# An LSTM step with a top-2 mixture of experts on one core: first half of expert 2's low weights added by DMA two token tiles sooner, two powers moved by a tile, a load and an output half on ScalarE's queue

## What is computed

```
def step(carry, xp_t):
    h_prev, c_prev = carry
    g = xp_t + h_prev @ u
    gates = jax.nn.sigmoid(g[:, :3 * H])
    c_cand = jnp.tanh(g[:, 3 * H:])
    ...
    c = fg * c_prev + ig * c_cand
    h = og * jnp.tanh(c)
x = _layernorm(x + _L0_attn_ref(x, w, u, bias), axis=-1)
...
dispatch, combine = _gating_top2(logits, C)
expert_inputs = jnp.einsum('GSEC,GSM->EGCM', dispatch, x)
layer_w0 = jnp.einsum('EGCM,EMH->EGCH', expert_inputs, w0_kernel)
layer_w1 = jnp.einsum('EGCM,EMH->EGCH', expert_inputs, w1_kernel)
hidden = jax.nn.gelu(layer_w0, approximate=True) * layer_w1
expert_outputs = jnp.einsum('EGCH,EHM->EGCM', hidden, wo_kernel)
out = jnp.einsum('EGCM,GSEC->GSM', expert_outputs, combine)
x = _layernorm(x + out, axis=-1)
```

## Time and profile before

| | us |
|---|---|
| median of 3 executions | 337.28 |
| lowest, highest | 336.99, 338.23 |
| the profiled execution | 338.06 |
| its span in the profile (first to last instruction) | 335.9 |
| busy in the span: PE, DVE, ACT, POOL | 287.1, 251.5, 217.8, 186.3 |
| mean granted clock of PE, as a share of full speed | 0.93 |

### The profile page before, as it was taken

One profiled execution on the slowest core, in us unless ns is written; L12 is line 12 of the kernel. 1 busy time (PEld: TensorE's weight loads), 2 busy tenths in 40 slices (PEclk: granted clock), 3 DMA queues, 4 the chain that ended last, 5 costly groups with the idle time before them and its releaser, 6 DMA issues.

```text
span 335.9 us, 5632 instructions
## 1 busy us (share of the span) xinstructions
PE 287.1 (85%) x1676; PEld 240.0 (71%) x1676; DVE 251.5 (75%) x805; ACT 217.8 (65%) x498; POOL 186.3 (55%) x154
## 2 busy tenths in 40 slices
PE   8999999968622996329999999999999999999990
PEld 5666665658611886229999987877888888889890
DVE  2799989987501894027888889989877777999985
ACT  4687987877421573026777876876765666669884
POOL 5015888788775027787864444347347337368700
PEclk9999999998985699557999999999999999999996
DMA  7996294478751005334444336264324224523664
GB/s 226 361 406 191 68 239 138 131 153 247 168 179 47 19 27 150 104 36 46 50 65 58 51 49 176 50 145 57 48 22 56 34 23 86 114 22 40 95 187 132
DMA packets 46828, 37.74 MB, mean 112 GB/s; under 512 B 7073, under 2 KB 40800, under 8 KB 46800
## 3 DMA queue, kind: packets, MB, share of 16 engines
q1 hardware_dynamic: 35392, 26.56, 26.8%
q0 software_dynamic: 11408, 10.85, 21.0%
HBM read 17.86 MB, written 17.10 MB: 104 GB/s over the span
## 4 chain that ended last, share of the span: by engine, by line
PE 71%; DVE 13%; issue 7%; another core or an unknown queue 5%; ACT 3%; ACTq 0%; POOL 0%; DVEq 0%; POOLq 0%
PE big L676 12%; PE big L674 12%; PE big L675 11%; PE big L582 5%; PE b_xnt L690 3%; PE b_xnt L693 3%; PE b_xnt L691 3%; PE b_ht L693 3%; PE b_ht L690 2%; PE b_ht L691 2%; PE b_rt L710 2%; PE b_xt L626 2%; PE big L568 1%; PE b_ht L631 1%
## 5 line engine op out<-in xcount | busy, mean ns | idle before, releaser
L878 ACT ACTIVATE act_g<-big 128x256 f32<-128x256 f32 (+1 forms) x144 | 65.4, 454 | 88.9 <-PE big L676 57.6
L674 PE MATMUL big<-x_hi,e_hi 128*128 128x256 f32 (+1 forms) x264 | 88.8, 336 | 4.1 <-issue 3.8
L675 PE MATMUL big<-x_hi,e_lo 128*128 128x256 f32 (+1 forms) x264 | 86.0, 326 | 0.0
L676 PE MATMUL big<-x_lo,e_hi 128*128 128x256 f32 (+1 forms) x264 | 86.0, 326 | 0.0
L511 POOL DMA_INDIRECT slots<-rows,slot_ix x64 | 66.3, 1035 | 35.5 <-issue 18.6
L526 POOL DMA_INDIRECT tokens<-contrib,token_ix x32 | 52.0, 1625 | 38.6 <-DVE token_ix L1169 30.6
L526 POOL DMA_INDIRECT tokens<-zero_rows,token_ix x28 | 45.6, 1629 | 32.9 <-DVE token_ix L1169 25.8
L674 PEld LDWEIGHTS big<-x_hi,e_hi 128*128 128x128 f32 x264 | 52.0, 197 | 8.0 <-issue 3.5
L676 PEld LDWEIGHTS big<-x_lo,e_hi 128*128 128x128 f32 x264 | 51.7, 196 | 4.0
L675 PEld LDWEIGHTS big<-x_hi,e_lo 128*128 128x128 f32 x264 | 52.0, 197 | 3.4
L1177 DVE TENSOR_TENSOR h<-act_g,big 128x256 f32<-128x256 f32 (+3 forms) x36 | 18.3, 509 | 18.8 <-ACT act_g L878 13.7
(11 more groups left out here) (212 smaller groups left out, 683.9 us busy)
## 6 DMA issues: line engine op xcount, KB each, us to landing
e_raw<-in_L_ffn_w_kernel_dram SPq DMA_DIRECT2D x16, 320.0 KB
slots<-zero_rows SPq DMA_DIRECT2D x8, 548.0 KB, 8.1
e_lo<-e_raw POOLq DMA_DIRECT2D x5, 544.0 KB
e_raw<-in_L_ffn_wo_kernel_dram SPq DMA_DIRECT2D x8, 320.0 KB
xd<-slots SPq DMA_DIRECT2D x16, 137.0 KB
xd<-slots SPq DMA_DIRECT2D x8, 274.0 KB
x<-in_L_attn_input_seq_dram SPq DMA_DIRECT2D x8, 256.0 KB, 4.6
tokens<-rows SPq DMA_DIRECT2D x8, 256.0 KB
```

What stands on the lines that cost most here:

```text
L674: pe.matmul(dst, e_hi[q][:, c0:c0 + m], xdt_hi[u % 2][:, 0:w], start=True, stop=False)
L675: pe.matmul(dst, e_lo[q][:, c0:c0 + m], xdt_hi[u % 2][:, 0:w], start=False, stop=False)
L676: mm = pe.matmul(dst, e_hi[q][:, c0:c0 + m], xdt_lo[u % 2][:, 0:w], start=False, stop=True)
L878: nc.scalar.activation(act0[n % RH][0:m, 0:w], pre(n, P)[0], ACT.Gelu_apprx_tanh).then_inc(gelu_ready, 1)
```

## The change

Five edits, by where they stand:

- On POOL the power of group 5 is issued two scatters later (before tile (1, 2) instead of (1, 1)), and the power of group 7 two scatters sooner (before (1, 5) instead of (1, 6)). The half of expert 2's low part that is made by DMA is issued four scatters sooner (before (1, 5) instead of (1, 7)).
- That half is now the first one (pieces 0 and 1), and DVE makes pieces 2 and 3. So ACT negates piece 0 in LSTM step 6 and piece 1 after chunk 4 of unit 0, instead of pieces 2 and 3 after chunk 5 of unit 0. DVE's first subtraction stays in LSTM step 7 (for piece 2 instead of 0); its second (piece 3, was 1) moves from after chunk 2 of unit 0 to after chunk 1 of unit 1.
- The load of `w_raw` is issued by ACT instead of SP.
- The outputs of groups 6 and 7 are stored in halves. SP stores the first half of 7, the first of 6 and the second of 7; ACT stores the second half of 6.
- Nothing is computed in another way, and PE's own list of instructions is the same.

```
-    NEGATIVE = {2: [(0, 0), (0, 1)], 4: [(1, 0)], 5: [(1, 1), (1, 2), (1, 3)]}
+    NEGATIVE = {2: [(0, 0), (0, 1)], 4: [(1, 0)], 5: [(1, 1), (1, 2), (1, 3)], 6: [(2, 0)]}
-    LOWS_AMONG = {(0, 3): (0, 1), (1, 2): (1, 0), (1, 3): (1, 1), (1, 7): (2, 1)}
-    ROOTS_AMONG = {(0, 3): 2, (0, 5): 3, (0, 7): 4, (1, 1): 5, (1, 3): 6, (1, 6): 7}
+    LOWS_AMONG = {(0, 3): (0, 1), (1, 2): (1, 0), (1, 3): (1, 1), (1, 5): (2, 0)}
+    ROOTS_AMONG = {(0, 3): 2, (0, 5): 3, (0, 7): 4, (1, 2): 5, (1, 3): 6, (1, 5): 7}
...
+        def half_out(g, h):
+
+            return out[g].rearrange("(t p) d -> p t d", p=P)[:, h * T // 2:(h + 1) * T // 2, :]
+
+        def half_fin(g, h):
+
+            return fin[g][:, h * T // 2:(h + 1) * T // 2, :]
...
-            sp.dma_start(w_raw[:, :], w_in[:, :]).then_inc(w_loaded, 16)
...
-            for g in range(S):
+            for g in range(LAST):
                 sp.wait_ge(fin_ready[g], T)
                 sp.dma_start(out[g].rearrange("(t p) d -> p t d", p=P), fin[g][:, :, :]).then_inc(out_done, 16)
-            sp.wait_ge(out_done, 16 * S)
+            for h in range(2):
+                for g in range(S - 1, LAST - 1, -1):
+                    if g == S - 1 or h == 0:
+                        sp.wait_ge(fin_ready[g], T // 2 * (h + 1))
+                        sp.dma_start(half_out(g, h), half_fin(g, h)).then_inc(out_done, 16)
+            sp.wait_ge(out_done, 16 * (S + GB))
...
+            act.dma_start(w_raw[:, :], w_in[:, :]).then_inc(w_loaded, 16)
...
-                    if (u, k) == (0, 5):
+                    if (u, k) == (0, 4):
+                        negative_weights(2, 1)
+                    elif (u, k) == (0, 5):
                         high_weights(2, 3)
-                        for n in range(PIECES // 2, PIECES):
-                            negative_weights(2, n)
...
+            act.wait_ge(fin_ready[LAST], T)
+            act.dma_start(half_out(LAST, 1), half_fin(LAST, 1)).then_inc(out_done, 16)
...
-                    low_weights(2, 0)
+                    low_weights(2, 2)
...
             chunk(0, 2)
-            low_weights(2, 1)
             chunk(0, 3)
...
             chunk(1, 1)
+            low_weights(2, 3)
             chunk(1, 2)
```

## The result

| | before | after |
|---|---|---|
| median of 20 executions each, us | 337.68 | 340.75 |
| ratio, with its 95% interval | | 1.0088 (1.0056 to 1.012) |
| profiled execution, us | 338.06 | 339.61 |
| its span, us | 335.9 | 337.5 |
| mean granted clock of PE | 0.93 | 0.926 |

A forecast was written before the change was run, and what follows sets the result against it. PE was taken as the bound except in two holes ending with POOL's scatter trains. POOL's 1.45 us plus 0.5 us at the end, 1.95 us off 337.28, gave 335.3 us, range 332.4 to 339.8.

The forecast's parts named there:

- The step that failed: PE's two idle stretches, about 84 to 109 and 126 to 151 us, were taken to end with POOL's scatter trains.
- the sum built on it: 1.45 us on POOL plus 0.5 us at the end, 1.95 us off the 337.28 median, giving 335.3 us.
- the rival "slower": POOL's train of 22 scatters, from about 76.6, opens the first hole sooner: 339.6 us, chance 0.20.
- the two signs: ACT's "remote" waits begin in unit 1, or PE's first dense stretch starts after 109.3 us.
- 4.3 us gross: 5.5 us of units 1 and 2, worth 4.4 chunks, would yield one: 3.4 chunks lost.
- The end: Final output stores: last issue 0.4 us sooner and half as large; 0.5 us gained, from 0.2 to 0.8.
- The start: Load of w_raw from ACT: SP's later loads some 0.45 us sooner, put at 0, range 0 to 0.4 us.
- POOL's shift: Power 5 no longer waits, so POOL's first scatter train ends 1.45 us sooner, between 1.1 and 1.8.
- unit 2 no longer held by `wait_low`: Expert 2's half lands by 82 us, so PE's 2.87 us idle before unit 2 at 88.90 goes.
- POOL did not wait for ACT's negation: Rival: POOL waits for ACT's piece 1 before issuing expert 2's half; 1 us of it gives 336.3, chance 0.04.
- the excess of its neighbours: Scatter beside power 5 took 0.52 us over the usual 0.98; if it and its neighbour lose this, about 1.8 us gained.
- The half of expert 2, put at nothing beyond POOL's shift: Issue moves from 82.37 to about 75.5; worth between nothing and 2.87 us, put at nothing since POOL sets the hole's end.

The follow-up runs named there:

- cutting that train once: Whole change plus one unused POOL power (1.16 us) ahead of tile (1, 7): 0.9977 of the kernel before.
- the kernels with pauses: Unused 1.1 us POOL powers ahead of every second tile of batches 2 and 3: changed kernel 0.916 and 0.9113, kernel before 0.9173 and 0.9234.
- The number of counts: Kernel before with one PE count instead of two for a chunk's first-layer products in small units: 0.9982.
- the fastest run: Changed kernel with a POOL memset of 330 columns ahead of every scatter from tile (1, 7) on: 303.29 us, 0.8969 of the kernel before.

## Why the prediction was wrong

**The step that failed** is the last one on what bounds the kernel, "I take it that a hole ends with POOL's train of scatters and not with anything on ACT, DVE or PE", together with the sum built on it. The sum valued how much sooner a train ends (1.45 us) and gave no price to how much sooner it begins. The train ended even sooner than I said (104.16, was 106.68, and I had put 105.2), but of these 2.5 us only 0.6 reached the end of the hole (108.69, was 109.28). But it began at 76.02, and the price of that stood only in the rival "slower", at 339.6 us with a chance of 0.20. Measured was 340.75. Of the two signs that I had named for it one came, the "remote" wait in unit 1 (97.38), and one did not: PE's dense stretch starts at 108.69, not after 109.3. The rival's place was right too: long waits in unit 1 and at the start of unit 2. It had said that a train of some 7 us makes counts late, from about 84 us; the first gelu behind its products is at 83.28, the first wait of over 3 us at 88.95. Its price, 4.3 us gross, compares with 5.0 (the 3.07 between the medians and the 1.95 of gains that I counted); cutting that train once gave 3.7 back, and this includes the 1.16 us that the pause itself takes on POOL.

I had argued against it that "the cut-up scatters at 70 to 80 us did not keep PE's counts prompt either". That was weak. A cut there costs POOL 1 us and brings the mean spacing down, and the kernels with pauses show that this is what counts.

**What held.**
- The end: ACT finishes group 6 at 334.40, and the span ends at 337.5, 3.1 us later. Before it was 332.25 and 335.9, 3.65 us. That is 0.55 us, and I had 0.5. The ends alone gave 0.9991, which agrees in sign and can't be told from nothing. The rows:

```profile
332.90 1.50 ACT L924 ACTIVATE x<-b_rt,root_b,root_y 128x128 f32<-128x128 f32 x4 [1.33 <-DVE root_b L1340]
334.44 0.48 ACTq L937 DMA_DIRECT2D out_dram<-x  x1
```

- The start: ACT rounds `w_raw` at 4.14, against 4.12 in the earlier trace rows. Nothing, as said.
- In the profiled execution, POOL's shift, unit 1 sooner by 1.06 us (I had 0.6), and unit 2 no longer held by `wait_low`.
- POOL did not wait for ACT's negation: the half is issued at 74.71 without idle time.

**What looks right and is not.** The two powers alone gave 0.9953, 1.6 us, and I had 1.45 for power 5 and the excess of its neighbours. That the numbers meet is luck. In that run POOL's first train ends at 106.83, against 107.35 with only the ends changed on the same chip, so 0.5 us sooner. Its DVE and POOL timelines show where the rest went:

```profile
62.51 0.69 DVE L956 SCALAR_TENSOR_TENSOR yd<-h,x 128x512 f32<-128x512 f32 x1 [1.37 <-remote]
```
```profile
68.77 1.42 POOL L491 TENSOR_TENSOR root_y<-root_x,minus_half 128x4 f32<-128x4 f32 x1 [1.77 <-DVE root_x L975]
```

By the code the DVE row waits for nothing but PE's logits of the group before, and PE had done them at 59.03. That is again a count of PE 3.5 us late, now in the LSTM: with power 5 moved, POOL issues six scatters in a row there (53.82 to 61.49) instead of four. DVE's variance of group 6 comes later by it, power 6 waits for it, and the lead of power 5 is gone. Of the 13 profiled executions of kernels with power 5 moved, 10 have this "remote" wait (0.7 to 1.4 us) and 11 have power 6 waiting (0.4 to 1.8 us); of the seven with power 5 in its old place none has either. The profile of the change itself is one of the two without both. So "all that follows on POOL is 1.12 us earlier at the least" fails in most executions. What gained the 1.6 us there stays open.

**What did not.** The half of expert 2, put at nothing beyond POOL's shift, costs 0.6% alone. Taking it from between the last scatters of batch 1 took away the break it made there. The rival named this break; the sum gave it no term. The range, 332.4 to 339.8, ended 1 us short of the median: of the slow case (338.5 to 341) it left out nearly half of the width, and not the quarter that I named.

**What stays open.** The runs show that PE's counts come late when POOL issues scatters densely, and that a wider spacing removes it, by work or by idleness. They don't show what is short: POOL's own path for descriptors, the DMA rings, or the memory the scatters write to. The DMA engines as a whole were not full: in the stretch from 89 us their share is 0.25 with the hole (77 GB/s) and 0.42 without it (120 GB/s). Nor do they show why PE's counts suffer and ACT's don't. The number of counts was ruled out. No run changed the size of a scatter's rows, which would tell the descriptors from the bytes.

## What to carry to other kernels

When an engine waits for counts that the producing engine earned long before, look at what the engine that issues DMAs is doing then: here the fix was to issue less densely, which made the kernel 8 to 10% faster where the change under study moved it by 1%. Ask of every step that sits between DMAs whether it is the break between them; moving it away may cost more than the step. And a stretch of waiting has a start as well as an end, and a term in the sum for each.

## What the runs showed of the hardware

- 64 indirect scatters from POOL of 128 rows each start 1.28 us apart when nothing stands between. In such a train gelus that need only PE's counts waited up to 12.1 us. With a 1.1 us power after every fourth scatter the changed kernel took 0.916 and 0.911 of the time of the kernel before, and with POOL waiting idle ahead of every tile 0.919.
- While PE's counts came 7 to 19 us late, ACT's reached DVE and PE 0.03 and 0.05 us behind the end of its instruction (at 107.67 and 98.11).
- 0.12 us of POOL work between two scatters changes nothing (1.0108, with 1.0088 for the change alone); 0.40 us, which brings the spacing to 1.55 us, gave 0.897 and 0.912 on two chips.
- PE's granted clock follows the holes: 0.50 in the stretch from 89 us of the changed kernel, the lower of its two levels (1.2 GHz), with PE busy for 5.64 us of the 9 before; 1.00 in the same stretch of the fastest run. At the high level first-layer matmuls start 0.12 us apart (from 82.30), at the low one 0.21 us (from 86.98). So a hole also makes the work that is left in it slower.
